# The last group of the attention stage takes over the start of the experts stage: two chunks, a transpose, the first shares and the Silu table

## The reference, cut to what matters

```python
x = _layernorm(x + _L0_attn_ref(x, ...))                 # a state space mixer
x = _layernorm(x + _L0_xattn_ref(x, ctx_1024, ..., mask)) # cross attention, 16 heads of 8
x = _layernorm(x + _L0_ffn_ref(x, ...))                  # 16 experts, 4 per token, and a shared one

# _L0_ffn_ref, cut (n tokens, h = 128, 64 hidden units per expert, 128 in the shared one)
scores = jax.nn.sigmoid(xf @ gate_w.T)
sfc = scores + gate_bias
...                                   # best 2 of 4 groups of experts, then the best 4 experts in them
cw = (jax.nn.one_hot(topk_idx, E) * topk_w[..., None]).sum(1)     # share of each expert, 16 per token
hg = jnp.einsum('nh,eih->nei', xf, Wg)
hu = jnp.einsum('nh,eih->nei', xf, Wu)
act = jax.nn.silu(hg) * hu
y = jnp.einsum('nei,ne,ehi->nh', act, cw, Wd)
shared = jax.nn.silu(xf @ Ws_g.T) * (xf @ Ws_u.T) @ Ws_d.T
return x + (y + shared).reshape(b, s, h)
```

## Time and profile before

| | us |
|---|---|
| median of 3 runs (lowest, highest) | 602.16 (601.14, 604.1) |
| the profiled execution's own time | 599.92 |
| its span, first to last instruction | 598.2 |
| mixer, from the start to the first scores of attention on PE | about 207 |
| attention, to the barrier | 207 to 404.7 |
| experts, from the barrier to the end | 404.7 to 598.2 |
| PE busy | 545.5 (91%) |
| DVE busy | 445.2 (74%) |
| ACT busy | 280.1 (47%) |
| POOL busy | 229.1 (38%) |

### The profile page before, as it was taken

How to read it: one execution, slowest core, us unless ns; L and a number is a source line. 1 busy time by engine, 2 the same in 40 slices (tenths; PEclk the granted TensorE clock), 3 DMA queues, 4 the chain that set the end, 5 groups by cost and what they waited for, 6 DMA issues and landing times. The chain is left out here.

```text
span 598.2 us, 17812 instructions
## 1 busy us (share of the span) xinstructions
PE 545.5 (91%) x6344; PEld 452.9 (76%) x6344; DVE 445.2 (74%) x1080; ACT 280.1 (47%) x556; POOL 229.1 (38%) x273
## 2 busy tenths in 40 slices
PE   5769999999999669999999999878999999999994
PEld 5748877787788547878778777767888888888883
DVE  3857877877798487778778787665796887877963
ACT  2358647756675316556556455533323323233220
POOL 2233546534753665244543546713022032131122
PEclk9979999999999958999999999998999999999998
DMA  7124232312332762654654455007246265165160
GB/s 217 38 99 124 76 97 75 122 53 90 102 119 65 200 184 77 185 143 128 173 149 122 136 142 168 7 5 177 65 115 143 63 150 132 60 164 128 38 157 18
DMA packets 55217, 67.42 MB, mean 113 GB/s; under 512 B 6705, under 2 KB 33104, under 8 KB 55152
## 3 DMA queue, kind: packets, MB, share of 16 engines
q1 hardware_dynamic: 52976, 63.58, 39.3%
q0 software_dynamic: 704, 1.92, 1.1%
q10 hardware_dynamic: 1472, 1.05, 0.8%
HBM read 49.26 MB, written 11.21 MB: 101 GB/s over the span
## 5 line engine op out<-in xcount | busy, mean ns | idle before, releaser
L1253 ACT ACTIVATE prob<-bank 128x512 f32<-128x512 f32 x128 | 69.4, 595 | 41.1 <-PE bank L1499 34.8
L2031 PE MATMUL bank<-xT_hl_c,w_up 128*128 128x512 f32 x288 | 85.9, 422 | 2.9 <-ACTq L67 2.9
L1948 ACT ACTIVATE sg<-bank 128x512 f32<-128x512 f32 x72 | 43.1, 598 | 95.2 <-PE bank L2031 89.7
L1349 DVE TENSOR_REDUCE nmax<-bank 128x4 f32<-128x512 f32 x112 | 71.9, 684 | 20.6 <-PE bank L1499 19.3
L2042 PEld LDWEIGHTS bank<-w_down,hid 128*128 128x128 f32 x576 | 73.9, 191 | 10.8 <-DVE hid L1988 3.7
L2042 PE MATMUL bank<-w_down,hid 128*128 128x128 f32 x576 | 76.4, 276 | 2.4 <-DVE res L124 1.5
L1489 PE MATMUL bank<-neg_i,mask 64*128 64x256 bf16 x512 | 52.1, 283 | 12.8 <-DMA q_stack<-q_scratch 4.3
L2031 PEld LDWEIGHTS bank<-xT_hl_c,w_up 128*128 128x128 f32 x288 | 50.2, 194 | 10.0 <-issue 3.1
L1988 DVE TENSOR_TENSOR hid<-gu,share 128x512 f32<-128x512 f32 x64 | 48.9, 763 | 6.0 <-DMA share<-cw_scratch 3.7
L1984 DVE TENSOR_TENSOR gu<-sg,bank_pair 128x512 f32<-128x512 f32 x48 | 32.8, 684 | 19.2 <-ACT sg L1948 13.2
L1747 POOL TENSOR_TENSOR xT_hl_c<-rest,xT_hl_c 128x512 fp32r<-128x512 f32 x7 | 9.0, 1285 | 94.4 <-ACT xT_hl_c L1728 94.4
(11 more groups left out here) (217 smaller groups left out, 1175.2 us busy)
## 6 DMA issues: line engine op xcount, KB each, us to landing
share<-cw_scratch SPq DMA_DIRECT2D x64, 256.0 KB, 5.5
rows<-sum_rows_scratch SPq DMA_DIRECT2D x32, 256.0 KB, 3.5
k_stack<-k_scratch SPq DMA_DIRECT2D x32, 128.0 KB, 2.8
q_stack<-q_scratch SPq DMA_DIRECT2D x32, 128.0 KB, 2.9
prev<-xnext SPq DMA_DIRECT2D x16, 224.0 KB, 2.5
k_scratch<-k_part SPq DMA_DIRECT2D x16, 192.0 KB, 2.4
q_scratch<-q_part SPq DMA_DIRECT2D x16, 192.0 KB, 2.5
x<-xT_in SPq DMA_DIRECT2D x8, 256.0 KB, 8.6
```

What stands on the lines that cost most here:

```text
L1253: act.activation(prob[:, b % 2, ORDER[n], :, :], (TT0, TT1)[n % 2][:, :], ACT.Exp, scale=XD ** -0.5)\
L1349: dve.tensor_reduce(nmax[:, b, 4 * u:4 * u + 4], (SS0, SS1)[n % 2][:, :].rearrange("p (i k) -> p i k", i=4), AX_X, ALU.max, negate=True).t ...
L1948: act.activation(sg[:, k, :], GG[k][:, :], ACT.Silu).then_inc(a_s.sem, 1)
L2031: mm = pe.matmul(bank[:, :], w_up[:, which, a, c, :], xT_hl[par][:, v, :], start=(n == 0), stop=(n == 2))
```

## The change

Work that the experts block did before its loop moves into the last group of attention, ahead of the barrier.

- PE: the transposes of x2 of group 1 come ahead of `spread_sums`, chunk 0's gate and up products between `spread_sums` and `output`, chunk 1's after `output`. The banks are the same ones, under attention's names (`TT0` and `TT1` are `GG[0]` and `GG[1]`, `SS1` and `U0` are `UU[0]` and `UU[1]`). Chunk 1 waits until ACT has copied the context out of `U0`.
- ACT: after the last context copy come `x2T_hi` of group 1 and one Silu of a 128x1 tile, ahead of which the table is loaded.
- SP: behind its last stack loads come the staging of x2 of group 1 and the 8 share DMAs of group 0, behind waits for the v projection of the last group, for x2 of group 1, for the stored shares and for the last use of the stacks.
- Memory: `xs` lies in attention's `cin`, `share` in the stacks `q_stack0` and `k_stack0`, the second x2 tile in `c_hl`. The semaphores concerned (`d_x`, `d_share`, `p_g`) are made and primed in attention.
- The wait of DVE for the last normalised x2, before ahead of the loop, stands before the first residual sum of the experts.
- POOL's low part of x2 of group 1, the two `silu` and the two `hidden` stay behind the barrier.

```diff
@@ attention, SP
+            for s in (e.d_x, *e.d_share):
+                s.prime(sp)
+            sp.sem_inc(e.d_x.sem[0], 16)
             sp.wait_ge(x1_out.sem, x1_out.at(NG - 1, 3))
             ahead(sp, group)
+            sp.wait_ge(p_v.sem, p_v.at(NG - 1))
+            sp.wait_ge(g_out.sem, g_out.at(1, 3))
+            stage_x2(sp, e, t, 1, 1)
+            sp.wait_ge(e.d_stored.sem, e.d_stored.at(0))
+            sp.wait_ge(p_t.sem, p_t.at(NG - 2, 4 * GS - 1))
+            for q in range(CHUNKS // 2):
+                load_share(sp, e, q, 0)
@@ attention, ACT, group
                 context(g)
                 if left:
                     store_max(g + 1, 1 - par, 1)
+                else:
+                    x2T_hi(act, e, 1, 1)
+                    act.activation(e.silu_table[:, :], e.bias[:, 0:1], ACT.Silu)
@@ attention, PE, group
+                else:
+                    turn_x2(pe, e, 1, 1)
                 spread_sums(g)
+                if not left:
+                    gate_and_up(pe, e, 0, 0, 0, (TT0, SS1))
...
                 output(g)
+                if not left:
+                    pe.wait_ge(a_ctx.sem, a_ctx.at(g))
+                    gate_and_up(pe, e, 0, 0, 1, (TT1, U0))
@@ expert_tensors
-    e.xT_hl = [sb("xT_hl_c0", [P, 2, GT], F32R)]
+    e.xT_hl = [sb("xT_hl_c0", [P, 2, GT], F32R), a.c_hl]
+    e.xs = a.cin[:, :, :].rearrange("p g (b t) -> p g b t", t=P)
+    e.share = [x[:, :, :, :].bitcast(F32).rearrange("p h c t -> p (h c t)").rearrange("p (c t) -> p c t", t=GT) for x in a.first]
+    e.silu_table = sb("silu_table", [P, 1])
...
+def turn_x2(pe, e, g, par):
+    pe.wait_ge(e.d_x.sem[par], e.d_x.at(g, par))
+    pe.wait_ge(e.a_c.sem, e.a_c.at(g - 1))
+    transpose_x2(pe, e, e.xs[:, par])
+
+def gate_and_up(pe, e, g, par, c, banks, freed=None):
+    if c == 0:
+        pe.wait_ge(e.v_x.sem, e.v_x.at(g))
+    for which, done in ((0, e.p_g), (1, e.p_u)):
+        if freed:
+            pe.wait_ge(freed[which].sem, freed[which].at(g, c - 3))
+        for n, (a, v) in enumerate(((0, 0), (0, 1), (1, 0))):
+            mm = pe.matmul(banks[which][:, :], e.w_up[:, which, a, c, :], e.xT_hl[par][:, v, :], start=(n == 0), stop=(n == 2))
+        mm.then_inc(done.sem, 1)
@@ experts
-            load(1, 1)
-            load_shares(0, 0)
             sp.wait_ge(x2_out.sem, x2_out.at(NG - 1, 3))
...
             silu(0, 0, 0)
             silu(0, 0, 1)
-            x2T_hi(act, e, 1, 1)
...
                 dve.wait_ge(p_d.sem, p_d.at(g, NC - 1))
+                if g == 0:
+                    dve.wait_ge(x2_out.sem, x2_out.at(NG - 1, 3))
                 residual_dve(dve, g, PO, ...)
...
             hidden(0, 0, 1)
-            dve.wait_ge(x2_out.sem, x2_out.at(NG - 1, 3))
...
-            up(0, 0, 0)
-            up(0, 0, 1)
-            x2T(1, 1)
             pairs(pe, group)
```

More of the change, by code:

```diff
@@ L1872, in experts @@
         hid = sb("hid", [P, NC, GT])
-        share = sb("share", [P, CHUNKS, GT])
         res, stats, mv, rstd = t["res"], t["stats"], t["mv"], t["rstd"]
@@ L1987, in hidden @@
                     dve.wait_ge(d_share[(c - 1) // 2].sem, d_share[(c - 1) // 2].at(g))
-                    dve.tensor_tensor(hid[:, c, :], gu[:, k, :], share[:, c - 1, :], ALU.mult).then_inc(v_hid.sem, 1)
+                    dve.tensor_tensor(hid[:, c, :], gu[:, k, :], e.share[(c - 1) // 4][:, (c - 1) % 4, :], ALU.mult).then_inc(v_hid.sem, 1)
             def group(g, par, left):
@@ L2016, in _ @@
         def _(pe):
-            for s in (p_g, p_d):
-                s.prime(pe)
-            def x2T(g, par):
-                pe.wait_ge(d_x.sem[par], d_x.at(g, par))
-                pe.wait_ge(a_c.sem, a_c.at(g - 1))
-                transpose_x2(pe, e, xs[:, par])
-            def up(g, par, c):
-                if c == 0:
-                    pe.wait_ge(e.v_x.sem, e.v_x.at(g))
-                for which, bank, freed, done in ((0, GG[c % 3], a_s, p_g), (1, UU[c % 3], v_gu, p_u)):
-                    pe.wait_ge(freed.sem, freed.at(g, c - 3))
-                    for n, (a, v) in enumerate(((0, 0), (0, 1), (1, 0))):
-                        mm = pe.matmul(bank[:, :], w_up[:, which, a, c, :], xT_hl[par][:, v, :], start=(n == 0), stop=(n == 2))
-                    mm.then_inc(done.sem, 1)
+            p_d.prime(pe)
+            def up(g, par, c):
+                gate_and_up(pe, e, g, par, c, (GG[c % 3], UU[c % 3]), (a_s, v_gu))
             def down(g, c):
@@ L2057, in group @@
                 if left == 2:
-                    x2T(g + 2, par)
+                    turn_x2(pe, e, g + 2, par)
                 down(g, NC - 2)
```

37 lines of the change are left out of this document (18 added, 19 removed).

## The result

The changed kernel has a median of 597.7 us in 11 runs (592.96 to 600.74), the kernel before 601.65 in the same series (599.13 to 604.1). The ratio is 0.992, with a 95% interval of 0.9894 to 0.9945: faster, by 0.55 to 1.06%. A second series of the same two gave 0.9905 (0.9875 to 0.9936). The profiled execution took 597.67, with a span of 595.9 against 598.2 before.

What follows compares the result with a forecast made beforehand. PE was taken to bound the experts stage, so its earlier logits, with full clock behind the barrier, give 4.9 us: median 602.16 - 4.9 = 597.3 us, range 595.3 to 600.0.

Steps and rivals of the forecast that it cites:

- What bounds: Experts stage: runs at PE's pace from its first logits to the end, so an earlier start moves the end equally.
- Transposes and output: PE before the barrier: transposes move `spread_sums` by 0.16, chunk 0's products delay `output` and the barrier by 0.71.
- The logits: PE behind the barrier: group 1's logits start at 405.9 instead of 410.77, gain 4.9, ends 4.5 and 5.2.
- Shares and table: ACT and SP before the barrier: table load covered by 2.2, share DMAs done at 404.5, 0.5 before DVE.
- Rival C: Attention's group 6: the staging copy adds up to 1.2 to PE's wait for `q_stack`; gain 3.7, 598.5; chance 0.04.
- Rival B: Experts' first chunks: DVE's `hid` slows beside POOL and falls behind PE; gain 3.3 to 4.4, 598.3; chance 0.10.
- Rival D: At the barrier: something else sets it and the removed work was covered; gain 0 to 1, 601.7; chance 0.08.
- Rival E: At the barrier: SP's share DMAs hold it, logits 1.8 later, half clock 1.7 more; slower, 605.7; chance 0.04.
- Rival A: PE's clock behind the barrier: low clock costs 1.47 to 1.7 of the gain, leaving 3.2 to 3.4; 598.9; chance 0.20.
- A's second form: Kernel before, timed runs: its clock did not fall, so 1.47 of the gain was never there; 0.20 for both forms.

Runs made afterwards that it cites:

- e9: Changed kernel with the staging copy late and the 12 products of chunks 0 and 1 back behind the barrier: 602.07 us, ratio 0.9991 to the kernel before.
- e4: Changed kernel with the staging copy late and all eight share DMAs back behind the barrier: 596.37 us, ratio 0.9907 to the kernel before.
- e3: Kernel before plus one unused 256 KB copy of group 1's x2, issued where the change stages it: 602.82 us, ratio 1.0005 to the kernel before.
- e2: Changed kernel with the staging copy issued later, in attention's last group: 595.52 us, ratio 0.9875 to the kernel before.
- e8: Changed kernel with staging copy late, group 1's logits ahead of the barrier, four of eight share DMAs behind it: 596.25 us, ratio 0.9882 to the kernel before.
- e12: Same kernel as e8, run again in another series: 594.0 us, ratio 0.9876 to the kernel before.
- e13: As e8 but with the staging copy early, as in the change: 597.87 us against 604.11, ratio 0.9888 to the kernel before.
- e1: The changed kernel again without edit, beside the kernel before: 597.5 us against 602.46, ratio 0.9905.
- late staging: Changed kernel with only the staging copy of x2 issued later, in attention's last group; run twice, ratios 0.9875 and 0.9898 to the kernel before.
- e11: Same kernel as e2, run again in another series: 595.51 us against 602.18, ratio 0.9898 to the kernel before.
- e5: Changed kernel with the staging copy late and the Silu table load back behind the barrier: 597.88 us, ratio 0.9915 to the kernel before.

## Why the prediction was right, and where a term was off

- **What bounds.** Right. From the first `down` to the end it took 184.32, before 185.02; what was won is the stream's earlier start. From the logits to the end, for which I had named 187.4, it took 188.17: 1.44 more for the clock, 0.70 less behind it.
- **Transposes and output.** Counted from the context products, `spread_sums` came at +1.48 (before +1.27), so 0.21 later, 0.16 predicted; `output` at +3.77 (before +3.20), 0.57 later, 0.71 predicted. DVE's statistics ended 0.46 later, POOL's first row came 0.48 later, 0.71 predicted. Chunk 1's products cost nothing, as said.
- **The logits.** Predicted 4.9 earlier, ends 4.5 and 5.2; measured 13.01 - 7.82 = 5.19. The barrier moved less than counted, and PE was at the logits 407.76 - 407.34 = 0.42 behind POOL, not 0.5. With the products behind the barrier (e9) the logits come after 12.98 again: this term stands or falls with the 12 products and the clock on them.
- **Shares and table, which I priced at nothing beyond the barrier.** The table is worth 0.07 in the seam and 0.17 at the eighth `down`. The shares, left behind, cost 1.7 at the eighth (e4), because DVE then asks before they land; ahead of the barrier they are there. So they win nothing alone (e9), but without them the gain would be 1.7 smaller.
- **Rival C, the staging copy.** The first trace spoke for it: 2.12 of waiting, then half clock. The runs don't: the copy alone gives 1.0005, and the wait ranges from 0.84 to 2.51 in the nine traces without it near and from 1.15 to 2.45 in the five with it. The last context products start at 394.86 to 401.97 in the nine and at 397.98 to 403.71 in the five, so the +2.18 of that execution is within the scatter. A small cost, under the 1.9 us that e3 leaves room for, is not excluded.
- **Rival B.** The delay of `hid` occurred (1.67 in e2) and PE didn't wait for it. One delay is covered, as worked out. In the changed kernel's own trace it didn't occur: the first `hid` took 0.69 at 409.33, in a stretch in which POOL was busy for 3.24 of 3.40 us. DVE became the limit only where the logits stood ahead too: 0.40 or 0.41 of waiting at chunk 5 in e8, e12 and e13.
- **Rival D.** Excluded by the seam, and by e9.
- **Rival E.** In small. I had given SP a cover of 0.5. It ended 0.35 before DVE in one execution, and since the barrier comes 0.76 behind SP's end but 0.41 behind DVE's, nothing of the cover was left; in another it ended with DVE and cost 0.4. Its issues don't wait for landings: these take 3.6 us at least in that trace, and POOL's row came 0.76 after SP's last. So it never came near 4.9.
- **Rival A, the clock: the step that failed.** "1.5 is nearer to the first, and I count with full clock behind the barrier." The pause was 1.59, and the clock fell: logits to first `down` 3.85, against 2.41 before, +1.44, the price I had given it. It fell in all three traces of kernels with this pause and the copy early (1.59, 1.97 and 1.57 idle) and in none of four with the copy late (1.51, 1.50, 1.51, 1.48), nor where the pause was 0.78 or 0.47. A describes the profiled executions: 5.19 - 1.44 = 3.75 won in the seam, 3.60 at the eighth `down` (3.20 in e1). With full clock, as counted, it would have been about the 5.26 of late staging. A's second form, that the kernel before often kept its clock, has no trace for it: the clock was low over the 12 products in all three traces that have them behind the barrier (before, e3, e9).

That the median came so near the forecast (597.7 against 597.3) is in part luck. The forecast stood on 602.16, 0.5 above the later median of the kernel before. From 601.65 it would have been 596.75, and rival A 598.35 in the middle of its range, with the measured 597.7 nearer to A. The gain was 3.95 by the medians of the 11 runs each, and 4.8 by the ratio of 0.992. In the trace the forecast missed 0.3 of gain at the barrier and lost 1.4 to the clock. A part of the timed runs may have kept the full clock; how many, the times alone don't tell. It also stays open whether the copy's place decides about the clock, directly or by those 0.06 of pause, or whether three against four traces is chance. The timed runs lean towards the copy's place (lower by 0.30 and 0.35 points in the two series above), and e13, early copy and full clock with the pause filled, fits either.

## What to carry to other kernels

When the stage behind a barrier runs at one engine's pace, ask of every piece of that engine's work behind it whether its inputs are there before, and put it into the waits ahead: here 12 products, and the logits with less gain. Follow the stream some chunks further than the seam, since the next engine's slack can take back what the seam won (0.8 of 1.16 here). Then list when each engine arrives, since the one that took over the DMA issues can become the last. Before a difference between two traces is laid to the change, run the suspected part alone: a wait of 2.12 that looked like the copy's came up as 2.51 without it.

## What the runs showed of the hardware that I had not expected

- PE's clock can fall well after the pause: in e1 the pause of 1.97 ended at 410.11, PE was then busy without a gap, the clock stayed at 1.00 until 412.0 and was 0.50 for the next 3.4 us. The six products behind the logits took 1.89 in place of 1.48, and the `down` products paid the rest.
- A pause of 1.5 to 1.6 went with full clock four times and with half clock twice. PE's wait for `q_stack` in group 6 shows the same spread in the 14 traces: a low stretch of 3.4 us begins at or soon after the end of waits of 1.71 (e9), 2.10, 2.12, 2.32, 2.45 and 2.51, and none does after the waits of 0.84 to 1.65, nor after 1.83 (e11). A nearest row is no guide between about 1.5 and 1.9.
- A table load of 1.28 behind a barrier delayed the first Silu by 1.29, its own length, in e5.
